# A recommender tower on one core: dots of a batch in one run, dense inputs inside the pairs, the first ids in a small load

## The reference

```python
e = jnp.stack([tbl_f[ids[:, f]] for f in range(32)], axis=1)   # 512 x 32 x 256
dots = jnp.einsum('bnd,bmd->bnm', e, e)
z = dots[:, iu, ju]                                            # upper triangle, 496
h = jnp.concatenate([z, dense_ctx], axis=1)                    # 512 x 512
h = jnp.maximum(h @ W_top1 + b_top1, 0.0)                      # 512
h = jnp.maximum(h @ W_top2 + b_top2, 0.0)                      # 256
y = h @ W_top3                                                 # 1
```

## Time and profile before

| | us |
|---|---|
| median of 3 runs | 173.32 |
| lowest, highest | 172.87, 173.36 |
| the profiled execution | 174.7 |
| its span, first to last instruction | 172.9 |
| PE busy | 144.4 |
| GpSimd busy | 110.1 |
| DVE busy | 67.9 |
| ACT busy | 60.0 |
| gathers, first and last start | 5.45, 147.69 |

### The profile page before, as it was taken

How to read it: one execution, slowest core, us unless ns; L and a number is a source line. 1 busy time by engine, 2 the same in 40 slices (tenths; PEclk the granted TensorE clock), 3 DMA queues, 4 the chain that set the end, 5 groups by cost and what they waited for, 6 DMA issues and landing times.

```text
span 172.9 us, 6157 instructions
## 1 busy us (share of the span) xinstructions
PE 144.4 (84%) x2768; PEld 117.1 (68%) x2768; DVE 67.9 (39%) x186; ACT 60.0 (35%) x140; POOL 110.1 (64%) x118
## 2 busy tenths in 40 slices
PE   0299999997799699898774999988843999988993
PEld 0188888885577578786653787867521888867991
DVE  0699685600124960065034401640254012668000
ACT  2543758443625412134312321125340121453111
POOL 1677787777777777777777777777777777300000
PEclk9999999999699999999997599999999699999999
DMA  5999999733434343333334343434333333300000
GB/s 126 311 374 373 346 350 338 240 112 96 121 96 126 96 118 102 110 110 104 111 101 116 97 119 95 119 98 117 102 111 106 102 113 99 88 4 4 4 0 2
DMA packets 10364, 23.14 MB, mean 134 GB/s; under 512 B 2881, under 2 KB 3009, under 8 KB 10338
## 3 DMA queue, kind: packets, MB, share of 16 engines
q0 software_dynamic: 5376, 14.69, 28.9%
q1 hardware_dynamic: 4674, 7.79, 13.5%
q10 hardware_dynamic: 288, 0.27, 0.6%
HBM read 22.73 MB, written 0.00 MB: 132 GB/s over the span
## 4 chain that ended last, share of the span: by engine, by line
PE 51%; POOL 22%; DMA 12%; issue 8%; ACT 4%; DVE 1%; ACTq 0%; DVEq 0%
POOL rows L209 22%; PE dots_ps L384 18%; PE mlp_ps L437 10%; DMA rows<-table,row_ids 9%; PE xt_ps L404 9%; PE dots_ps L426 5%; PE xt_ps L437 3%; DMA chunk_rows_sb<-chunk_rows 3%; PE mlp_ps L457 2%; PE mlp_ps L432 2%; ACT h L315 1%; PE dots_ps L457 1%; ACT kept L287 1%; ACT xt L293 1%; DVE one_hot L224 1%
## 5 line engine op out<-in xcount | busy, mean ns | idle before, releaser
L209 POOL DMA_INDIRECT rows<-table,row_ids x112 | 109.4, 977 | 37.8 <-issue 32.0
L404 PE MATMUL xt_ps<-ident,rows 128*128 128x128 f32 x224 | 41.3, 297 | 13.7 <-DMA rows<-table,row_ids 11.5
L293 ACT COPY xt<-xt_ps 128x512 f32<-128x512 f32 (+1 forms) x36 | 20.8, 577 | 82.1 <-PE xt_ps L404 82.1
L234 DVE COPY xt<-xt_ps 128x512 f32<-128x512 f32 (+1 forms) x28 | 15.6, 558 | 78.7 <-PE xt_ps L404 78.7
L404 PEld LDWEIGHTS xt_ps<-ident,rows 128*128 128x128 f32 x224 | 25.8, 147 | 21.1 <-DMA rows<-table,row_ids 10.2
L426 PEld LDWEIGHTS dots_ps<-xt 128*32 128x32 f32 x2048 | 23.4, 116 | 12.6 <-issue 12.4
L426 PE MATMUL dots_ps<-xt 128*32 128x32 f32 x2048 | 30.1, 204 | 1.9 <-issue 1.9
L437 PE MATMUL mlp_ps<-pairs,small_sb 128*128 128x128 f32 x208 | 31.3, 297 | 0.0
L244 DVE COPY pairs<-dots_ps 32x128 f32<-32x128 f32 (+1 forms) x108 | 29.1, 269 | 2.4 <-PE dots_ps L426 0.8
L384 PE MATMUL dots_ps<-one_hot,high 128*128 128x512 f32 x64 | 21.6, 420 | 7.7 <-DVE low L228 7.7
L437 PEld LDWEIGHTS mlp_ps<-pairs,small_sb 128*128 128x128 f32 x208 | 26.6, 201 | 1.0
(11 more groups left out here) (27 smaller groups left out, 42.1 us busy)
## 6 DMA issues: line engine op xcount, KB each, us to landing
small_sb<-small_tables SPq DMA_DIRECT2D x16, 256.0 KB, 8.6
small_sb<-w SPq DMA_DIRECT2D x8, 256.0 KB, 8.2
rows<-table,row_ids POOLq DMA_INDIRECT x112, 2.8
small_ids_sb<-small_ids SPq DMA_DIRECT2D x3, 256.0 KB, 8.6
small_sb<-w SPq DMA_DIRECT2D x1, 512.0 KB, 4.3
small_ids_sb<-small_ids ACTq DMA_DIRECT2D x1, 256.0 KB, 4.4
ids_sb<-ids SPq DMA_DIRECT2D x1, 112.0 KB, 4.1
w1d_sb<-w1d SPq DMA_DIRECT2D x1, 32.0 KB, 8.3
```

What stands on the lines that cost most here:

```text
L209: nc.gpsimd.indirect_dma_start(rows[:, slot, :], None, table, bass.IndirectOffsetOnAxis(ap=row_ids[:, m * GATHERS + t:m * GATHERS + t + 1] ...
L234: nc.vector.tensor_copy(*fill_parts(n, u)).then_inc(xt_dve, 1)
L293: nc.scalar.copy(*fill_parts(n, u)).then_inc(xt_act, 1)
L404: last = nc.tensor.transpose(xt_ps[at_fill % 3][:, at:at + P], rows[:, slot, c * P:(c + 1) * P], ident[:])
```

## The change

- **First ids.** A small array first_ids holds chunk_rows and the ids and bases of batch 0 (22 words per partition). It is loaded first; DVE adds 14 columns and GpSimd may start batch 0. The ids of batches 1 to 15 are loaded behind the first chunk of the first small table and added behind DVE's first low part; GpSimd waits for them ahead of batch 1. ACT no longer loads chunk_rows.
- **Dense inputs.** Column 0 of the first 32 partitions of pairs has no pair above the diagonal. DVE zeroes it once, the moves leave it out, and the 16 dense inputs of a block are loaded there; their weights stand in the same place of w1. dense_sb, w1d_sb and 16 dense products are gone. The loads of blocks 2 and 3 wait until layer 1 of blocks 0 and 1 has read the place.
- **Dots.** A batch's 64 products stand in one run behind fill 0 of the next batch, instead of in quarters behind its four fills.
- **Moves.** A unit's moves stand behind fill 1 (DVE also 2) of the batch that follows its second batch. In the last batch the moves are split differently: of the unit's first batch DVE moves three quads and ACT one behind fill 1, of its second both move two.
- **Network.** Layer 1 of block 0 starts two slots earlier, of blocks 1 and 2 three slots earlier, so that layers 2 and 3 of block 2 stand ahead of the last dots.

```diff
-ROUND = {"layer1": [2, 3, 4, 5, 6, 7, 8, 9], "relu1": 10, "layer2": [11, 12], "relu2": 13, "layer3": 14, "keep": 15}
+LAST_QUADS = range(2), range(2, QUADS)
+DOTS_BEHIND = [10, 13]
+ROUND = {"layer1": [0, 1, 2, 3, 4, 5, 6, 7], "relu1": 8, "layer2": [9, 10], "relu2": 11, "layer3": 12, "keep": 13}
...
+        first_sb = sb("first_sb", [P, CHUNKS + 2 * GATHERS], I32)
+        chunk_rows_sb = first_sb[:, 0:CHUNKS].bitcast(F32)
+        first_ids_sb = first_sb[:, CHUNKS:].rearrange("p (h i) -> p h i", h=2)
+        ids_sb = sb("ids_sb", [P, 2, (NM - 1) * GATHERS], I32)
...
             for q in range(QUADS):
-                to = pairs[Q * q:Q * (q + 1), b % 2, :, at + first * GROUPS:at + last * GROUPS]
-                source = dots_ps[v % 2][Q * s:Q * (s + 1), first:last, :, q * JJ:(q + 1) * JJ]
+                skip = int(q == 0)
+                to = pairs[Q * q:Q * (q + 1), b % 2, skip:, at + first * GROUPS:at + last * GROUPS]
+                source = dots_ps[v % 2][Q * s:Q * (s + 1), first:last, :, q * JJ + skip:(q + 1) * JJ]
...
-                at = (n - (BATCHES * b + FIRST + 1)) * FILLS + u
+                at = (n - BATCHES * (b + 1)) * FILLS + u - (FILLS if b == 0 else FILLS - 1)
...
-            sp.dma_start(ids_sb[:], ids).then_inc(ids_in, 16)
+            sp.dma_start(first_sb[:], first_ids).then_inc(first_in, 16)
...
+                    if k == c == 0:
+                        sp.dma_start(ids_sb[:], ids).then_inc(ids_in, 16)
...
-            sp.dma_start(w1d_sb[:], w1d).then_inc(weights_in, 16)
-            sp.dma_start(dense_sb[:], dense).then_inc(weights_in, 16)
+            def load_dense(b):
+                sp.dma_start(pairs[0:dense.shape[0], b % 2, 0, :],
+                             dense[:, b * BLOCK:(b + 1) * BLOCK]).then_inc(dense_in, 16)
+
+            sp.wait_ge(no_pairs_zeroed, 1)
+            load_dense(0)
+            load_dense(1)
...
+            for b in range(2, NB):
+                sp.wait_ge(l1_done, N1 * (b - 1))
+                sp.wait_ge(dense_in, 16 * b)
+                load_dense(b)
...
             for m in range(NM):
+                if m < 2:
+                    pool.wait_ge(ids_ready, m + 1)
...
-            dve.wait_ge(ids_in, 16)
-            nc.vector.tensor_tensor(row_ids[:], ids_sb[:, 0, :], ids_sb[:, 1, :], ALU.add).then_inc(ids_ready, 1)
+            nc.vector.memset(pairs[0:Q, :, 0, :], 0.0).then_inc(no_pairs_zeroed, 1)
+            dve.wait_ge(first_in, 16)
+            nc.vector.tensor_tensor(row_ids[:, 0:GATHERS], first_ids_sb[:, 0, :], first_ids_sb[:, 1, :],
+                                    ALU.add).then_inc(ids_ready, 1)
...
                     take_xt(n, u)
-                    if n % 2 and n > FIRST + 1:
-                        if u == 0:
-                            move((n - 3) // UNIT, range(2), last=False)
-                        if u == 1:
-                            move((n - 3) // UNIT, range(2, DVE_QUADS), first=False)
-            v = NM // UNIT - 1
-            move(v, range(DVE_QUADS), (0, 1))
-            move(v, range(DVE_QUADS), (1, UNIT))
+                    if n % UNIT == 0:
+                        if u == 1:
+                            move(n // UNIT - 1, range(2), last=False)
+                        if u == 2:
+                            move(n // UNIT - 1, range(2, DVE_QUADS), first=False)
+                    if n == NM - 1 and u == 1:
+                        move(n // UNIT, range(DVE_QUADS), (0, 1))
+            move(NM // UNIT - 1, LAST_QUADS[0], (1, UNIT))
...
             for n in range(FIRST + 1, NM):
                 for u in range(FILLS):
                     fill(n, u)
-                    dots((n - 1) * GROUPS + 2 * u, (n - 1) * GROUPS + 2 * u + 2)
+                    if u == 0:
+                        dots(n - 1)
                     mlp(n, u)
-            m, last = NB - 2, NB - 1
-            dots((NM - 1) * GROUPS, NM * GROUPS)
-            for u in range(FILLS):
-                mlp(NM, u)
-            for k in range(N1 - 1):
-                dense_part(last, k, last_l1_ps, start=True)
-            pairs_complete(last)
+            dots(NM - 1)
...
+    w1[0, 0:dense.shape[1], 0] = W1[len(iu):]
```

More of the change, by code:

```diff
@@ L32, with build_tower @@
 DVE_QUADS = 3
+LAST_QUADS = range(2), range(2, QUADS)
 FIRST = 4
 FILL_BEHIND = [2, 4, 5, 7, 8, 10, 11, 13, 14]
-ROUND = {"layer1": [2, 3, 4, 5, 6, 7, 8, 9], "relu1": 10, "layer2": [11, 12], "relu2": 13, "layer3": 14, "keep": 15}
-def build_tower(nc, table, ids, small_tables, small_ids, chunk_rows, dense, w1, w1d, b1, w2, b2, w3, out):
+DOTS_BEHIND = [10, 13]
+ROUND = {"layer1": [0, 1, 2, 3, 4, 5, 6, 7], "relu1": 8, "layer2": [9, 10], "relu2": 11, "layer3": 12, "keep": 13}
+def build_tower(nc, table, first_ids, ids, small_tables, small_ids, dense, w1, b1, w2, b2, w3, out):
     D = table.shape[1]
@@ L47, in build_tower @@
     N1, N2 = H1 // P, H2 // P
-    KR, CHUNKS = chunk_rows.shape
+    KR, CHUNKS = small_tables.shape[1:3]
     assert KR == P
@@ L104, in build_tower @@
         last_l3_ps = found_ps[1][0][0:1, 0:BLOCK]
+        first_in = sem("first_in")
         ids_in = sem("ids_in")
@@ L351, in _ @@
                         take_kept(n)
-                        if n % 2 and n > FIRST + 1:
-                            move((n - 3) // UNIT, range(DVE_QUADS, QUADS))
+                        if n % UNIT == 0:
+                            move(n // UNIT - 1, range(DVE_QUADS, QUADS))
+                        if n == NM - 1:
+                            move(n // UNIT, range(DVE_QUADS, QUADS), (0, 1))
                     for b, at in slots(n, u):
@@ L360, in _ @@
                             keep_y(b, loop_ps[0][0:1, :])
[L361 to L364, removed]
+            b = NB - 1
             keep_y(b - 1, loop_ps[0][0:1, :])
+            move(NM // UNIT - 1, LAST_QUADS[1], (1, UNIT))
             for k in range(N1):
@@ L406, in fill, with dots @@
                 last.then_inc(transposed, 1)
[L408 to L421, removed]
+            def dots(n):
+                v = n // UNIT
+                on_act, on_dve = moved_fills(n, FILLS - 1)
+                pe.wait_ge(xt_act, on_act)
+                if on_dve:
+                    pe.wait_ge(xt_dve, on_dve)
+                pe.wait_ge(kept_in_xt, n + 1)
+                if n % UNIT == 0 and v >= 2:
+                    pe.wait_ge(moved_act, v - 1)
+                    pe.wait_ge(moved_dve, v - 1)
+                for g in range(GROUPS):
                     to = dots_ps[v % 2][:, n % UNIT, g, :]
@@ L427, in dots, with pairs_part @@
                                                     start=(c == 0), stop=(c == DC - 1))
[L428 to L435, removed]
+                done.then_inc(dots_done, 1)
+            def pairs_part(b, n, columns, bank):
                 for j in columns:
-                    done = nc.tensor.matmul(banks[n], w1_sb[:, j, n * P:(n + 1) * P], pairs[:, b % 2, j, :],
-                                            start=(start and j == 0), stop=(stop and j == JJ - 1))
-                return done
-            def pairs_complete(b):
-                more = b == NB - 1
-                pe.wait_ge(moved_dve, 2 * (b + 1) + more)
-                pe.wait_ge(moved_act, 2 * (b + 1) + more)
+                    done = nc.tensor.matmul(bank[n], w1_sb[:, j, n * P:(n + 1) * P], pairs[:, b % 2, j, :],
+                                            start=(j == 0), stop=(j == JJ - 1))
+                return done
             def layer1_half(b, i):
                 if i == 0:
-                    pairs_complete(b)
+                    pe.wait_ge(moved_dve, UNIT * (b + 1))
+                    pe.wait_ge(moved_act, UNIT * (b + 1))
+                    pe.wait_ge(dense_in, 16 * (b + 1))
                     if b:
                         pe.wait_ge(y_ready, b)
-                pairs_part(b, i // 2, range(i % 2 * JJ // 2, (i % 2 + 1) * JJ // 2), loop_ps)
+                done = pairs_part(b, i // 2, range(i % 2 * JJ // 2, (i % 2 + 1) * JJ // 2), loop_ps)
                 if i % 2:
-                    dense_part(b, i // 2, loop_ps).then_inc(l1_done, 1)
+                    done.then_inc(l1_done, 1)
             def layer2(n, k, banks):
@@ L487, in _ @@
             pe.wait_ge(found_kept, LOOKED_UP)
-            between = FIRST * FILLS - len(FILL_BEHIND)
-            for i in range(between):
-                fill(*divmod(len(FILL_BEHIND) + i, FILLS))
-                dots(2 * GROUPS * i // between, 2 * GROUPS * (i + 1) // between)
+            for f in range(len(FILL_BEHIND), FIRST * FILLS):
+                fill(*divmod(f, FILLS))
+                if f in DOTS_BEHIND:
+                    dots(DOTS_BEHIND.index(f))
             for u in range(FILLS):
                 fill(FIRST, u)
-                dots(2 * GROUPS + 4 * u, 2 * GROUPS + 4 * (u + 1))
-            pe.wait_ge(weights_in, 16 * (JJ + 3))
+                if u % 2 == 0:
+                    dots(len(DOTS_BEHIND) + u // 2)
```

(1 more changed line is left out.)

35 lines of the change are left out of this document (19 added, 16 removed).

## The result

| | us |
|---|---|
| before, median | 173.09 (172.54 to 173.36) |
| changed kernel, median of 4 | 177.85 (177.24 to 178.72) |
| ratio | 1.028, 95% interval 1.022 to 1.035 |
| span profiled, before and after | 172.9 and 176.5 |

A forecast was written before the change was run, and what follows sets the result against it. It took PE's work to bound the last 20 us, with GpSimd's gathers landing the last row at about 150.5. Layer 1 of the last block 5.3 us earlier gave 174.7 - 5.3 = 169.4, taken as 168.9; range 167.2 to 171.3.

The forecast's parts named there:

- part 2: PE up to the last fill: net 3.2 us less work, more than its 2.3 us lateness, so last fills wait for rows.
- The first gather, 0.8 earlier: Start of GpSimd's gathers: a small first ids load lets them begin 0.8 us earlier, between 0 and 1.45.
- the rival of a quicker load: First ids load quicker than any transfer traced: gain 2.1 us instead of 0.8, time 167.6; chance 0.10.
- PE waits for rows again before the last fills: Batch 15's last fills: PE waits for gathered rows, the last dots ending near 152.3 to 152.8.
- the sum: Whole kernel: profiled 174.7 us less 5.3 gives 169.4; 168.0 if profiling adds a constant; 168.9 taken.
- the term of the early network: Layer 1 of block 2 on PE, three fill slots earlier: puts 3.3 us into the idle time of 124 to 133.5.
- Part 3: Moves and dense loads: PE could wait 0.2 us for DVE's moves at layer 1, costed at nothing because of slack.
- the first rival: End of kernel: PE's clock falls around the wait for moves, 3.4 us at 1.2 GHz lose 1.6: 170.5; chance 0.22.
- slower: End of kernel: clock falls at the wait for moves and stays low over the tail, losing 7.4 us: 176.3; chance 0.06.
- Four mechanisms: The rivals: clock falls at the end (0.22), PE stays late (0.14), quicker small load (0.10), clock low through the tail (0.06).

The follow-up runs named there:

- E3: Changed kernel with dots in quarters behind the four fills, moves and network in their old places; 172.21 us, 0.998 of the kernel before.
- halves: Changed kernel with a batch's dots in the loop cut into 64 records behind fill 0 and 64 behind fill 1; 169.45 us, 0.981 of the kernel before.
- E4: The run of halves: changed kernel, dots cut into two lots of 64 records, moves and network early; 169.45 us, ratio 0.981.
- E12: Halves of dots with moves and network back in the places of the kernel before; 172.14 us, 0.997 of the kernel before.
- E10: Halves, with DVE moving two quads of samples instead of three and ACT the other two; 170.24 us, 0.978 of the kernel before.
- E11: Halves, with layers 1 and 2 one slot later; 169.09 us, 0.984 of the kernel before.
- E9: Changed kernel with the second half of every dot product left out, 64 records per run in the same place; 168.40 us, 0.980 of the kernel before.
- E6: Changed kernel with 1024 more dot records behind the last dots; 288.15 us, one run, not comparable; the added passes took 30.5 us.

## Why the prediction was wrong

The step that failed stands in part 2: "A batch's dots were four pieces of 0.39 us, 1.56; in one run the same 128 records take 1.30, so two batches save 0.5." The 1.30 was measured once, on the only full run of before, which crossed a border of two pieces without a stop. The term had no price for the supply of instructions. In the loop a run of 256 instructions meets a border every time, and it stops there when it gets to the border less than 2.2 to 2.8 us after the packet's start. What was to save 0.25 us per batch cost stops of 9.3 us in the dots and 2.6 at layer 1, and then the waits for DVE and ACT behind them. R as I had put it, that a run uses up a piece in 1.2 us before the next arrives, is too narrow. PE was in its piece for 1.5 to 2.7 us before the stops up to 65 us, for 2.3 and 3.1 before those at 89.95 and 118.33, and for 5 and more before those at 125.30 and 152.08, where the packet came only after a wait for a semaphore. What these stops share is a stretch of short instructions that reaches the border while the packet is still on its way.

The timeline of before had the hint, and I did not read it: stops on "issue" of 0.9 and 1.0 us ahead of 56.66 and 60.29, in the one stretch of that kernel with many dots and little else. The weight loads' 12.4 us on "issue" in its view of waits are no such hint: E3, without runs, has 13.7.

The other steps, one by one:

- *The first gather, 0.8 earlier*: 0.34 (5.11 against 5.45); the load took 3.91 us from its issue to DVE's start against 4.15. Small size hardly helped; the 3.91 also put aside the rival of a quicker load (2.0 us). The last gather came 0.97 earlier all the same: by the eleventh the lead had grown to 0.95 (18.80 against 19.75), and it stayed so (the sum of GpSimd's busy time fell by 0.7).
- *PE waits for rows again before the last fills*: wrong in the changed kernel, where fill 3 of batch 15 ran at 156.7, 7 us behind its rows. Right in halves. Its timeline, with the rows forecast in part 2 (fill 3, layer 3, dots, moves, layer 1 of the last block; compare):

```profile
150.99 0.41 PE L433 MATMUL xt_ps<-ident,rows 128*128 128x128 f32 x2 [1.48 <-DMA rows<-table,row_ids]
151.33 0.60 PE L487 MATMUL mlp_ps<-h,w_sb 128*1 128x128 f32 x4
...
151.96 1.29 PE L455 MATMUL dots_ps<-xt 128*32 128x32 f32 x128
...
153.28 1.81 DVE L273 COPY pairs<-dots_ps 32x56 f32<-32x56 f32 x8 [1.43 <-PE dots_ps L455]
155.15 3.84 PE L462 MATMUL xt_ps<-pairs,small_sb 128*128 128x128 f32 x32 [1.90 <-DVE pairs L273]
```

  I had layer 1 at 154.65 and find 155.15; the wait for the moves 1.9 and find 1.90. The profiled execution of halves took 169.5 us, and the sum had 169.4. That it fits so closely is in part luck: layer 1 began 0.5 us late (the first gather's 0.8 was 0.34), and the tail from there took 12.4 instead of 12.8. E4 and E12 bear out the term of the early network together with that of the early moves, 2.7 us of the 3.4 between forecast and before; which of the two brings it with halves was not tested.
- *Part 3, 0.2 us for the moves, hidden*: 6.5 us in two waits in the changed kernel, because PE came late and did its fills in one go; 2.3 us in halves, and what these cost is too little for E10 and E11 to tell.
- *The rivals*: none of them was this one. The clock did fall at the wait for the moves as the first rival said: the first 32 records of the last layer 1 took 5.39 us there against 3.84 in halves, 1.5 us as it had priced. But a low clock alone did not make the kernel slow: E9 has more of it.
- *The chances*: I gave 0.06 to slower, all of it to the clock, with 6.8 us as the longest low stretch traced; the changed kernel has one of 10.3 us (90.7 to 101.0). Four mechanisms that could only differ in size left no room for a resource that no view had been read for.

By place, the loss can be read off the two traces. The last fill starts 5.7 us later than in halves (156.7 against 151.0), where halves waits for rows and the changed kernel does not; the last layer 1 begins 7.4 later (162.54 against 155.15); its first 32 records take 1.5 longer at the low clock; and the span ends 8.9 later. How these divide by cause I did not separate: the stops as waits make 11.9 us, part of each falls into what is slack in halves, and part comes back through the low clock (31 us at the low level in the changed kernel, 21 in halves by the mean clock of 0.937) and the waits for DVE and ACT.

The Trainium skill, "Runtime: NRT & Kernel Launch", section "Instruction fetch mechanics", says that an engine's instructions come in blocks of 16 KiB, 256 instructions, through a queue of their own, and that crossing a block's border is mostly hidden. The traces agree on the blocks: 22 packets in 0.36 MB on the instruction queue, and in E6 stops 128 records apart. They do not agree that it is hidden: 3.77 us per block in E6 where PE needs 1.2 to 1.9 for its contents.

## What to carry to other kernels

Instructions are a resource with a rate: in a long run of small products, 256 of PE's in 3.8 us. A record of the dots is two instructions for 10 ns of work (1.30 us for 128), so a run of them outpaces the supply at every border. What worked here was to cut it and lay it between fills, which use few instructions for their time (10 records in 1.3 us). When work is gathered into longer runs, read the "issue" waits of that line in the timeline and the packets of the instruction queue first, and price a run at the supply, not at its best single occurrence. A run behind a wait for a semaphore is at risk too: at three places here, 149.8 among them, the packet with the next piece started only after that wait. And when one part of a bundled change goes wrong, test the parts in a square: here one line cost 8 us, the early moves and network were worth 2.7 once it was mended, and the other parts, about 1 us at most together, could not be told from nothing.

## What the hardware showed that I had not expected

- The supply of PE's instructions: a packet of 16 KB takes 0.9 to 1.4 us, work resumes 1.2 to 1.6 us after its end, and in runs of dots pieces follow each other every 3.5 to 4.0 us at either clock. Only one piece is fetched ahead, and its packet starts after PE has entered the piece before, in 18 of 22 cases within 2.1 us.
- A load of 11 KB, the first on its queue, took 3.9 us from its issue to DVE's start, nearly what 112 KB took in the same place (4.15).
- One comparison ran in a condition where the kernel before took 241.6 us instead of 173, at a mean clock near 0.80, and two variants of halves, elsewhere 2% faster, were 6 to 7% slower, at 0.74 to 0.77. What that condition was stays open.
